# Adding up the squares of the masked scores by accumulating transfers begun from GpSimd, in an adjacency-masked attention kernel

## What is computed

```python
# x: (16, 1024, 512) f32, adj: (1024, 1024) of 0 and 1
q = jnp.einsum('bnd,ed->bne', x, Wq)
k = jnp.einsum('bnd,ed->bne', x, Wk)
v = jnp.einsum('bnd,ed->bne', x, Wv)
rel = jnp.einsum('bnd,bmd->bnm', q, k)
rel = adj.T[None, :, :] * rel
rel = rel / jnp.linalg.norm(rel, axis=2, keepdims=True)
x = layernorm(x + jnp.einsum('bnm,bmd->bnd', rel, v))
```

## Time and profile before

| | |
|---|---|
| time, median of 3 runs | 1971.78 us (1971.39 to 1971.95) |
| profiled execution: its own time | 1971.97 us |
| profiled execution: its span, first to last instruction | 1970.2 us |
| mean granted clock of TensorE | 0.997 |
| PE busy | 1957.0 us (99%) |
| DVE, POOL, ACT busy | 1531.9 (78%), 957.8 (49%), 762.5 us (39%) |
| DMA engines, mean busy share | 40.2%, all of it from SP's queue |

### The profile page before, as it was taken

One profiled execution on the slowest core, in us unless ns is written; L12 is line 12 of the kernel. 1 busy time (PEld: TensorE's weight loads), 2 busy tenths in 40 slices (PEclk: granted clock), 3 DMA queues, 4 the chain that ended last, 5 costly groups with the idle time before them and its releaser, 6 DMA issues.

```text
span 1970.2 us, 28685 instructions
## 1 busy us (share of the span) xinstructions
PE 1957.0 (99%) x9857; PEld 1669.1 (85%) x9857; DVE 1531.9 (78%) x2085; ACT 762.5 (39%) x1288; POOL 957.8 (49%) x639
## 2 busy tenths in 40 slices
PE   8999999999999999999999999999999999999998
PEld 6888888888888888888888888888888888888887
DVE  8796877868778696787968779687796877868775
ACT  5433434335342352423424234342433424335341
POOL 5744536455354553446435374453644536455352
PEclk9999999999999999999999999999999999999999
DMA  5734343344524345343444333443434343344401
GB/s 188 314 134 165 144 167 115 144 154 154 186 92 149 142 157 184 122 151 118 157 175 160 128 139 133 172 153 128 160 128 170 144 155 127 144 154 152 185 26 64
DMA packets 80416, 292.22 MB, mean 148 GB/s; under 512 B 7441, under 2 KB 7441, under 8 KB 76305
## 3 DMA queue, kind: packets, MB, share of 16 engines
q1 hardware_dynamic: 80400, 292.06, 40.2%
HBM read 251.13 MB, written 40.89 MB: 148 GB/s over the span
## 4 chain that ended last, share of the span: by engine, by line
PE 97%; DVE 1%; POOL 1%; DMA 0%; issue 0%; SPq 0%; ACT 0%; POOLq 0%; DVEq 0%
PE banks L422 32%; PE banks L424 32%; PE banks L423 32%; DMA scr<-xT 0%; DVE aw L794 0%; DVE x_lo L755 0%; POOL scr L1063 0%; DVE yv L816 0%; POOL square_sum L1067 0%; POOL squares L1067 0%; SPq L344 0%; POOL scr L1072 0%; SPq L343 0%; POOL res L1075 0%; POOL res L1080 0%
## 5 line engine op out<-in xcount | busy, mean ns | idle before, releaser
L422 PE MATMUL banks<-yv 128*128 128x512 f32 x1024 | 399.8, 390 | 0.0
L424 PE MATMUL banks<-yv 128*128 128x512 f32 x1024 | 398.5, 389 | 0.0
L423 PE MATMUL banks<-yv 128*128 128x512 f32 x1024 | 398.5, 389 | 0.0
L1119 POOL TENSOR_TENSOR square_sum<-square_sum,squares 128x512 f32<-128x512 f32 x224 | 319.9, 1428 | 85.7 <-ACT squares L657 75.1
L422 PE MATMUL banks<-yv,x_hi 128*128 128x512 f32 x896 | 348.7, 389 | 0.5 <-DVE rel L857 0.5
L424 PE MATMUL banks<-yv,x_lo 128*128 128x512 f32 x896 | 348.6, 389 | 0.0
L423 PE MATMUL banks<-yv,x_hi 128*128 128x512 f32 x896 | 348.6, 389 | 0.0
L1136 POOL TENSOR_TENSOR rstd<-var_eps,minus_half 128x1 f32<-128x1 f32 x128 | 144.2, 1127 | 329.3 <-DVE var_eps L968 329.3
L423 PE MATMUL banks<-aw,x_hi 128*128 128x256 f32 x896 | 253.6, 283 | 0.0
L424 PE MATMUL banks<-aw,x_lo 128*128 128x256 f32 x896 | 253.5, 283 | 0.0
L422 PE MATMUL banks<-aw,x_hi 128*128 128x256 f32 x896 | 253.5, 283 | 0.0
(11 more groups left out here) (108 smaller groups left out, 3430.5 us busy)
## 6 DMA issues: line engine op xcount, KB each, us to landing
scr<-adj SPq DMA_DIRECT2D x128, 512.0 KB, 5.8
aw<-w_kept SPq DMA_DIRECT2D x16, 3584.0 KB, 11.1
aw<-a_kept SPq DMA_DIRECT2D x15, 3584.0 KB, 11.0
scr<-xT SPq DMA_DIRECT2D x32, 1024.0 KB, 7.1
res<-x SPq DMA_DIRECT2D x128, 256.0 KB, 2.7
out<-res SPq DMA_DIRECT2D x128, 256.0 KB, 2.0
a_kept<-aw SPq DMA_DIRECT2D x1, 3584.0 KB, 18.2
w_kept<-v_raw SPq DMA_DIRECT2D x3, 512.0 KB, 8.5
```

Source lines behind the costliest of these rows:

```text
L422: pe.matmul(bank_ap, l_hi, r_hi, start=first and i == 0, stop=False, skip_group_check=on)
L423: pe.matmul(bank_ap, l_hi, r_lo, start=False, stop=False, skip_group_check=on)
L424: mm = pe.matmul(bank_ap, l_lo, r_hi, start=False, stop=i == len(pairs) - 1, skip_group_check=on)
L1119: pool.tensor_tensor(square_sum[:, h, :], square_sum[:, h, :], squares[:, n % SQRING, :], ALU.add).then_inc(square_added, 1)
```

## The change

POOL no longer adds. It begins, for each n, a transfer from the ring slot into `square_sum[:, h, :]` that adds what it carries to what stands there. Each transfer counts 16 on a semaphore of its half when it has landed, so there are two semaphores now. Before POOL begins transfer n it waits until the transfer before it of the same half has landed (`behind`), since two that add to the same bytes may not overlap. ACT waits for the transfer of n - 2, by the semaphore of that one's half, and `turn_squares` waits for both. POOL's loop over the batches is written out 16 times.

```diff
-        square_added = sem("square_added")
+        square_added = [sem(f"square_added{h}") for h in range(2)]
...
-        ADDED = len(added_order)
+        behind = {s: sum(half_of[o[0]] == half_of[s[0]] for o in added_order[:n]) for n, s in enumerate(added_order)}
+        ADDED = DMA * len(added_order) // HALVES
...
-                    act.wait_ge(square_added, b * ADDED + (n + 1))
+                    if n >= SQRING:
+                        before = added_order[n - SQRING]
+                        act.wait_ge(square_added[half_of[before[0]]], b * ADDED + DMA * (behind[before] + 1))
                     target = squares[:, n % SQRING, :]
...
             def turn_squares(b):
-                dve.wait_ge(square_added, b * ADDED + (ADDED + SQRING))
+                for h in range(HALVES):
+                    dve.wait_ge(square_added[h], b * ADDED + ADDED)
...
-            pool.sem_inc(square_added, SQRING)
...
             def add_square(b, name, i):
                 n = added_order.index((name, i))
                 h = half_of[name]
+                if behind[name, i]:
+                    pool.wait_ge(square_added[h], b * ADDED + DMA * behind[name, i])
                 pool.wait_ge(squared, b * SQUARES + (square_order.index((name, i)) + 1))
-                pool.wait_ge(square_added, b * ADDED + (n + SQRING))
-                pool.tensor_tensor(square_sum[:, h, :], square_sum[:, h, :], squares[:, n % SQRING, :],
-                                   ALU.add).then_inc(square_added, 1)
+                pool.dma_start(square_sum[:, h, :], squares[:, n % SQRING, :],
+                               accum_op=ALU.add).then_inc(square_added[h], DMA)
...
-            with pool.Fori(0, B - 1) as b:
-                batch(b, False)
-            batch(B - 1, True)
+            for b in range(B):
+                batch(b, b == B - 1)
```

## The result

The changed kernel takes 2193.74 us (median, 2192.53 to 2196.26), the kernel before, measured beside it, 1971.87 us. The ratio is 1.113, with an interval of [1.111, 1.114]: 222 us slower, where 192 were forecast. The profiled execution has a span of 2194.5 us, 224.3 more than before.

The account below looks back on a forecast made before the run. TensorE, busy 1957.0 of 1970.2 us, was taken to bound the kernel. Per batch 10.4 us for the chain plus 1.6 for the clock gave 12.0, times 16 is 192, so 1971.97 + 192 = 2164 us, range 2030 to 2325.

Parts of the forecast that it names:

- POOL's relief is worth nothing: Whole kernel: TensorE doesn't wait for POOL's 224 additions (319.9 us), so taking them off POOL gains nothing.
- The chain through the halves: Per batch, seven transfer prices, five POOL holds and 2.65 us of masking in series make `turn_squares` 10.4 us late.
- g = 1.0: Time for which one transfer holds POOL: taken as 1.0 us, bounds 0 and 1.4.
- The price c = 4.5: Time from POOL's start of one transfer until the next of its half may start: taken as 4.5 us.
- Which path ends last: At the output, DVE allows the first output product at 962.8, 1.4 us after TensorE's v products end at 961.4.
- the copies' path: In ACT's queue, squares waiting for landings delay `v_copy(0)` and `v_copy(1)`; the v products behind them end at 961.4.
- The stops and the clock: In each batch's v stage TensorE stands still 6.0 and 3 us; half clock afterwards adds 1.6 us.
- Sixteen equal batches: Every batch loses the same 12.0 us, 16 x 12.0 = 192 us in all.
- the one wait of TensorE in the s stage: Sign, in the trace after: the prediction is wrong if TensorE also waits in the s stage.
- The cheap transfer: Rival: a transfer price of 2.8 us or less hides entirely, 1972 us; chance 0.07, and 0.09 for 2.8 to 3.5.
- The much dearer transfer: Rival: a transfer price above 6 us, from loads or slow adding; at 7 us, 2444 us; chance 0.10.
- stay low through the v stage: Rival: TensorE's clock stays low, nine v products at 2.9 us end 22 us late, 2324 us; chance 0.06.

Follow-up runs that it names:

- The late load of x: Changed kernel with the next batch's x load, and the mask loads behind it, begun only after all 14 transfers of the batch landed: 2098.49 us.
- copies_first: Changed kernel with both copies of the first v results put ahead of the last three squares in ACT's queue: 2199.78 us.
- fillers: Changed kernel with 36 unused matmuls per batch where TensorE waits for the first copy: 2190.02 us.
- plain transfers: Changed kernel with each transfer only copying its 256 KB and adding nothing: 2097.54 us.

## Why the prediction was right, point by point

**That POOL's relief is worth nothing** held, and was shown by itself: 1972.07 us without the additions.

**The chain through the halves** held step by step: c follows c where two of a half follow each other, POOL's hold follows where the half changes, and the maskings of m22 stand in it. g = 1.0 was 0.7 to 0.9, from the start of one transfer to that of the next; POOL is held for 0.88.

**The price c = 4.5** was right only as a mean over unlike steps. Away from the load of x it was 4.0 to 4.6, 4.3 in the mean of five, and in it 10.4. From n = 2 to the start of n = 13 the sum had 34.65 us (6c + 5g + 2.65); the batch took 1062.47 - 1023.75 = 38.7. The text did say that the last transfers meet the loads, but spread that as 0.3 us over all. This is the term that was mis-sized: about +6 us for one step and -0.2 for each of the others. The late load of x shows it, 95 us for 15 batches.

**Which path ends last.** DVE's path was to end 1.4 us behind TensorE's. They end together: DVE's turning follows at once on its work before it, and in six batches TensorE waits a little for DVE at the output. `copies_first` showed that with the copies' path cleared DVE's alone gives the same time; the copies' path alone was not run.

**The stops and the clock.** 6.0 and 3.1 us of standing still became 9.3 and 0.9, since n = 10, for which the first copy waits, is the dear one. The half clock was there for some 8 us of work. The 1.6 us that the sum added for it were not confirmed as a cost of their own: with fillers 4 us of 222 came back. In the middle batches the squares are turned 13.1 us late and the batch is 13.4 us longer, so about 0.3 are left for it. That 13.4 came so near to 12.0 is therefore partly luck: 10.4 for the chain was 2.7 too low and 1.6 for the clock 1.3 too high.

**Sixteen equal batches** was wrong in a way that nearly cancels. The middle ones lost 13.4 us and not 12.0; the last, without a load of x, 7.5; the first 29.1. In the first, n = 2 to n = 3 alone took 13.0 us (70.77 to 83.77), beside the 3.5 MB load of the v weights, which there is issued at 68.15 only. That is argued from the trace; no run moved that load. There, too, lies the one wait of TensorE in the s stage, which the text had named as a sign of being wrong: 1.6 us, in this batch alone.

**The rivals.** The cheap transfer fell: at 4.0 us at the least c is past the 2.8 from which it costs. Where the price was under 2.8, with plain transfers in the last batch, the chain did hide but for 0.3 us. The much dearer transfer came true for the one step among the loads and for no other. The clock did not stay low through the v stage: in the batch shown it was back within some 8 us of work. The Trainium skill's formula ("DMA: Bandwidth & Descriptors", "Anatomy of one DMA") gives 2.6 us for 256 KB and, with both operands counted, 3.2. From start to landing, with no other transfer in flight, the plain one took 2.3 us and the adding one 3.3; start to start, as the chain pays it, they took 2.6 and 3.6 to 4.6. The sum needs the second price, and for a transfer that adds it is well above the formula's.

## What to carry to other kernels

An operation that an idle engine does in 1.4 us is not made cheaper by a transfer that the engine begins: the hold falls to 0.9 us, but whoever needs the result waits 4 us, and in a chain where each waits for the last (one sum, one buffer) every step pays that. Before handing small work to the DMA engines, count the steps that depend on each other, and look up which large loads are in flight at each of them: one step among 3 MB of loads cost here as much as nearly two and a half others. The wait that the profile names is not yet the gain: here two paths hung on the same chain, and clearing the first only showed the second.

## What the runs showed of the hardware that was not expected

- How long a transfer takes behind large loads goes by what was issued ahead of it and hardly by its own size. Start to start, the second of a pair took 4.4 us with no load in flight, 8.4 with 2 MB issued in the 4 us ahead of it and 10.4 with 3 MB; with 2 MB ahead, adding only 128 KB still took 8.0 to 9.1. The Trainium skill says that each DMA engine takes turns between the queues ("DMA: Bandwidth & Descriptors", "SWDGE vs HWDGE vs iDMA"); with even turns between two queues the step would hardly grow with what stands in one of them, and here it grew by about 2 us for each MB. What sets the order stays open.
- Of two transfers in flight together the second takes longer and the first does not, though they touch different bytes. In the batch shown of the kernel with the late load of x, n = 8 alone and n = 9, the first of a pair, both landed 3.3 us after their start, n = 10 behind it 3.9 us after its own. Start to start one alone took 3.6 to 3.7 us (n = 8 in the two kernels with the late load, in the batches shown) and the second of a pair 4.4 to 4.5 (n = 10 and n = 12).
- DVE's masking from two operands in SBUF (L895, L903) took 1127 and 1320 ns in the mean with POOL's additions beside it and 685 and 684 ns without them. The Trainium skill ("SBUF — State Buffer", "Who interferes with whom") says that such an operation and a GpSimd one that reads SBUF exclude each other, and the trace agrees. Here it moved 66 us of DVE's time and none of the kernel's.
